# Four graph layers on one core: the last layer in groups of four blocks, shorter ends of the gathering passes, and the last product in rows

## What is computed

```
h = relu(layernorm(x)); x = x + layer0(h)  # sum of neighbours, product 256->512, batch norm, relu, product ->256, batch norm, relu
h = relu(layernorm(x)); x = x + layer1(h)  # two weighted sums over edges (in and out), gates
h = relu(layernorm(x)); x = x + layer2(h)  # sum of neighbours, products 256->256->256 with batch norms
h = relu(layernorm(x)); x = x + layer3(h)

# layer3, for each edge (src, tgt):
feat = concat(x[tgt], x[src] - x[tgt])
hid  = relu(feat @ W1 + b1)                # 512 wide
msg  = hid @ W2 + b2                       # 256 wide
out  = segment_sum(msg, tgt) / (deg + 1e-8)
```

## Time and profile before

| | us |
|---|---|
| median of three runs | 3542.32 |
| the profiled execution | 3547.39 |
| its span | 3545.6 |
| TensorE matmul busy | 2770.3 (78%) |
| GpSimd busy | 2368.3 (67%) |
| VectorE busy | 2055.5 (58%) |
| ScalarE busy | 1146.7 (32%) |

### The profile page before, as it was taken

How to read it: one execution, slowest core, us unless ns; L and a number is a source line. 1 busy time by engine, 2 the same in 40 slices (tenths; PEclk the granted TensorE clock), 3 DMA queues, 4 the chain that set the end, 5 groups by cost and what they waited for, 6 DMA issues and landing times.

```text
span 3545.6 us, 57073 instructions
## 1 busy us (share of the span) xinstructions
PE 2770.3 (78%) x12116; PEld 1910.4 (54%) x12117; DVE 2055.5 (58%) x6142; ACT 1146.7 (32%) x3033; POOL 2368.3 (67%) x2444
## 2 busy tenths in 40 slices
PE   4999866666875766667999676666668889999999
PEld 2444444444434444445777444444444469999996
DVE  7999833443455544445444546444444488888883
ACT  1999700000142010000000014000003457777772
POOL 5777777777777777777777733777771046666661
PEclk6999977777886777877999887777778899999999
DMA  4000033333214333333333313333331157777774
GB/s 146 2 2 2 3 105 104 104 104 104 59 41 153 97 105 104 104 106 105 104 104 102 104 51 95 105 104 104 105 104 30 66 172 214 214 210 216 213 215 127
DMA packets 168186, 381.37 MB, mean 108 GB/s; under 512 B 53443, under 2 KB 78094, under 8 KB 168131
## 3 DMA queue, kind: packets, MB, share of 16 engines
q0 software_dynamic: 123264, 321.84, 31.6%
q1 hardware_dynamic: 44867, 58.89, 5.0%
HBM read 352.65 MB, written 27.84 MB: 107 GB/s over the span
## 4 chain that ended last, share of the span: by engine, by line
PE 44%; issue 22%; POOL 16%; DMA 11%; DVE 4%; DVEq 1%; ACT 1%; POOLq 0%; ACTq 0%; SPq 0%
PE psum L1926 17%; PE psum L2189 11%; POOL acc L771 9%; POOL recs L747 7%; DMA acc<-table,stg_idx 6%; PE psum L2177 6%; PE psum L2101 4%; DMA recs<-acc,sst_idx 3%; PE psum L1947 2%; DVE acc L1336 1%; DVEq L528 1%; PE psum L2146 1%; DMA recs<-acc 1%; DVE oh L1325 1%; PE psum L2128 1%
## 5 line engine op out<-in xcount | busy, mean ns | idle before, releaser
L771 POOL DMA_INDIRECT acc<-table,stg_idx x1568 | 1501.3, 957 | 492.9 <-issue 437.7
L1926 PE MATMUL psum<-acc,oh 128*128 x3520 | 1228.5, 501 | 595.6 <-SPq L611 266.3
L1926 PEld LDWEIGHTS psum<-acc,oh 128*128 128x128 f32 x3520 | 817.2, 248 | 987.1 <-issue 857.4
L1336 DVE TENSOR_TENSOR acc<-acc,psum 128x257 f32 (+1 forms) x880 | 371.3, 422 | 889.5 <-PE psum L1926 881.5
L921 ACT CAST stg_idx<-rec 128x2 int32 (+1 forms) x784 | 149.3, 193 | 1790.2 <-PE psum L1926 1766.3
L841 POOL DMA_INDIRECT TT<-qtable,stg_row x440 | 419.8, 954 | 188.8 <-issue 166.2
L1327 DVE TENSOR_SCALAR oh<-iota,stg_lw 128x128 f32<-128x128 f32 x1320 | 404.3, 363 | 133.1 <-issue 133.0
L2189 PEld LDWEIGHTS psum<-oh,TT 128*128 128x128 f32 x3520 | 427.9, 192 | 19.4
L2189 PE MATMUL psum<-oh,TT 128*128 128x128 f32 x3520 | 429.0, 275 | 0.0
L747 POOL DMA_INDIRECT recs<-acc,sst_idx x290 | 305.4, 1053 | 120.1 <-issue 86.0
L1996 PE MATMUL psum<-H 125*128 125x440 bf16 x1600 | 314.0, 350 | 14.5 <-ACT H L874 13.2
(11 more groups left out here) (256 smaller groups left out, 2571.4 us busy)
## 6 DMA issues: line engine op xcount, KB each, us to landing
acc<-table,stg_idx POOLq DMA_INDIRECT x1568
table<-H SPq DMA_DIRECT2D x12, 640.0 KB
TT<-loc_dram SPq DMA_DIRECT2D x22, 320.0 KB, 5.1
TT<-qtable,stg_row POOLq DMA_INDIRECT x440
Wm<-loc_dram SPq DMA_DIRECT2D x22, 320.0 KB, 4.9
qtable<-H SPq DMA_DIRECT2D x24, 256.0 KB, 2.0
recs<-acc,sst_idx POOLq DMA_INDIRECT x290, 2.1
recs<-rec SPq DMA_DIRECT2D x5, 880.0 KB, 5.7
```

Source lines behind the costliest of these rows:

```text
L771: pool.indirect_dma_start(out=dst[:, c, 0:D], out_offset=None, in_=src, in_offset=bass.IndirectOffsetOnAxis(ap=stg_idx[:, c:c + 1], axis=0 ...
L1336: V.tensor_tensor(at, at, sum_bank(j)[:, 0:w], ALU.add).then_inc(added, 1)
L1926: last = mm(sum_bank(j)[:, 0:w], oh[:, 2 * j + k, :], rows_flat[:, ds(start[j] + k * S, w)], start=(k == 0), stop=(k == 1))
```

## The change

Three parts. (1) The last turn of each narrow pass is written out; its last pair of gathers is one gather of END_ROWS = 80 rows, and `relay` and its counts follow. (2) The norm of layer 3, its transposes, the q products and the addition of the bias go in groups of four blocks, interleaved in the programs of TensorE, VectorE and ScalarE; all 25 q blocks come before the p blocks; back2 has banks 3, 4 and 5; the second memset of H is cut into three, of which two (5376 columns) run once q is stored and one (1024 columns) after the last p block. (3) "down3" and "back3" give way to "out3": H is the stationary operand and W2 the moving one, so that a result is a block in rows, 25 x 4 matmuls of 256 columns; ScalarE's copies go.

```
 def relay(n):
-    with sp.Fori(n * GITS, (n + 1) * GITS) as i:
+    short = [0] * (RING_G - 1) + [16]
+    with sp.Fori(n * GITS, (n + 1) * GITS - 1) as i:
         for j in range(RING_G):
-            sp.wait_ge(landed[j], i * 32 + 32)
+            sp.wait_ge(landed[j], i * 32 + (32 - n * short[j]))
             sp.sem_inc(arrived, 1)
+    for j in range(RING_G):
+        sp.wait_ge(landed[j], (n + 1) * GITS * 32 - (n + 1) * short[j])
+        sp.sem_inc(arrived, 1)
 # GpSimd, gathers(n, src, dst)
-    with pool.Fori(n * GITS, (n + 1) * GITS) as i:
+    with pool.Fori(n * GITS, (n + 1) * GITS - 1) as i:
         for j in range(RING_G):
             gather_pair(i, j, src, dst)
+    for j in range(RING_G - 1):
+        gather_pair((n + 1) * GITS - 1, j, src, dst)
+    pool.wait_ge(staged, (n + 1) * GITS * RING_G)
+    pool.sem_inc(stages_begun, 1)
+    c = 2 * RING_G - 2
+    pool.indirect_dma_start(out=dst[0:END_ROWS, c, 0:D], out_offset=None, in_=src,
+        in_offset=bass.IndirectOffsetOnAxis(ap=stg_idx[0:END_ROWS, c:c + 1], axis=0)
+    ).then_inc(landed[RING_G - 1], 16)
 # GpSimd, clearing H
-    all_filled("p3")
-    nc.gpsimd.memset(Hm[:, NB * D:4 * NP], 0.0).then_inc(sums_clear, 1)
+    all_filled("q3")
     for q in range(QS):
         pool.wait_ge(q_stored[q], 16 * (NB // QS))
+    p_half = w0 + 2 * HID
+    nc.gpsimd.memset(Hm[:, NB * D:w0], 0.0).then_inc(sums_clear, 1)
+    nc.gpsimd.memset(Hm[:, p_half:4 * NP], 0.0).then_inc(sums_clear, 1)
+    all_filled("p3")
+    nc.gpsimd.memset(Hm[:, w0:p_half], 0.0).then_inc(sums_clear, 1)
 # ScalarE
+    for g in range(len(TG) + 3):
+        n = 2 * (NB // GROUP) + g + 2
+        if g < len(TG): deviations(n, 4 * g, len(blocks_of(g)))
+        if 1 <= g <= len(TG): norm_blocks(n - 1, 4 * (g - 1), len(blocks_of(g - 1)))
+        if 2 <= g <= len(TG) + 1: take_transpose(3, g - 2)
+        if g >= 3:
+            for t in blocks_of(g - 3): take_q(t)
 # VectorE
+    for g in range(len(TG) + 2):
+        n = 2 * (NB // GROUP) + g + 2
+        if g < len(TG): ln_rows(blocks_of(g), "back2").then_inc(ln_var, 1)
+        if 1 <= g <= len(TG):
+            done = blocks_of(g - 1)
+            ln_scale(n - 1, slice(done.start, done.stop))
+        if g >= 2:
+            take_transpose(3, g - 2)
+            full_rows(blocks_of(g - 2))
 # TensorE
+    back_rows(0)
+    back_rows(1)
     for g in range(len(TG) + 1):
+        if g + 2 < len(TG): back_rows(g + 2)
         if g < len(TG): transpose_group(3, g)
         if g >= 1:
             for k in (0, 1): wait_emptied(pe, "T3", 2 * (g - 1) + k)
-        for t in blocks_of(g - 1):
-            if t < Q_FIRST: rows_product("q3", t, 2)
+            for t in blocks_of(g - 1): rows_product("q3", t, 2)
     pe.wait_ge(wdiff, 1)
     for t in range(NB):
         rows_product("p3", t, 0)
-        if Q_FIRST + t < NB: rows_product("q3", Q_FIRST + t, 2)
...
-    for n in range(NT):
-        products("down3", n, 2, [(W2e[:, k, :], H_at(k, n)) for k in range(4)], n * 2)
-        back("back3", u_ready, lambda n: NT + 2 * (n + 1), ended_by(n - 1))
-    back("back3", u_ready, lambda n: NT + 2 * (n + 1), ended_by(NT - 1))
+    for t in range(NB):
+        r = rows(t)
+        dst = take_bank("out3", t)
+        for k in range(4):
+            last = mm(dst[0:r, 0:D], H[:, k, t * P:t * P + r], W2e[:, k, :], start=(k == 0), stop=(k == 3))
+        done(last, "out3", t)
```

More of the change, by code:

```diff
@@ L35 @@
 HB = 2
+END_ROWS = E - (GROUPS - 1) * EDGES
+assert 0 < END_ROWS <= P and END_ROWS % 16 == 0
 assert EP * EC == E and CHUNKS % (2 * CH_IT) == 0 and CHUNKS % 4 == 0 and CH_IT % HB == 0
@@ L62 @@
 MID = N // 2
-Q_FIRST = 16
 PFS = 3
@@ L502, in gnn_kernel @@
         plan("down2", 2 * NT)
-        plan("back2", NB)
+        plan("back2", NB, (3, 4, 5))
         plan("T3", 2 * len(TG), (6, 7))
@@ L506, in gnn_kernel @@
         plan("p3", NB, (3, 4, 5))
-        plan("down3", 2 * NT, range(4))
-        plan("back3", NB, range(4, 8))
+        plan("out3", NB)
         def blocks_of(g):
@@ L1057, in take_q @@
                 nc.scalar.copy(qst[0:rows(t), t % QS, :], src[0:rows(t), :]).then_inc(emptied[bank("q3", t)], 1)
-            for g in range(len(TG) + 1):
+            for g in range(len(TG) + 3):
+                n = 2 * (NB // GROUP) + g + 2
                 if g < len(TG):
-                    take_transpose(3, g)
-                for t in blocks_of(g - 1):
-                    if t < Q_FIRST:
+                    deviations(n, 4 * g, len(blocks_of(g)))
+                if 1 <= g <= len(TG):
+                    norm_blocks(n - 1, 4 * (g - 1), len(blocks_of(g - 1)))
+                if 2 <= g <= len(TG) + 1:
+                    take_transpose(3, g - 2)
+                if g >= 3:
+                    for t in blocks_of(g - 3):
                         take_q(t)
@@ L1256, in ln_stats, with ln_rows @@
             def ln_stats(g, back=None):
+                return ln_rows(range(g * GROUP, (g + 1) * GROUP), back)
+            def ln_rows(blocks, back):
                 stats = []
-                for t in range(g * GROUP, (g + 1) * GROUP + 2):
-                    if back is not None and t < (g + 1) * GROUP:
+                for t in range(blocks.start, blocks.stop + 2):
+                    if back is not None and t < blocks.stop:
                         add_back(back, t)
-                    if g * GROUP <= t - 1 < (g + 1) * GROUP:
+                    if t - 1 in blocks:
                         r = rows(t - 1)
@@ L1268, in ln_stats @@
                         stats.append(nstep[0])
-                    if g * GROUP <= t - 2:
+                    if t - 2 in blocks:
                         r = rows(t - 2)
-                        dve.wait_ge(vstep, stats[t - 2 - g * GROUP])
+                        dve.wait_ge(vstep, stats[t - 2 - blocks.start])
                         last = V.bn_aggr(lnmv[0:r, t - 2, :], lnst[0:r, (t - 2) % (2 * GROUP), :])
@@ L1301, in add_back, with take_transpose @@
                     emptied[bank(st, t)], 1)
+            def take_transpose(layer, g):
+                st = f"T{layer}"
+                src = wait_filled(dve, st, 2 * g + 1)
+                n = min(512, N - 512 * g)
+                V.tensor_copy(TT[:, 1, 512 * g:512 * g + n], src[:, 0:n]).then_inc(emptied[bank(st, 2 * g + 1)], 1)
             def take_transposes(layer):
@@ L1684, in _, with full_rows @@
             bn_scale(5, 2, "L2_gnn_g2", "L2_gnn_be2")
[L1685 to L1695, removed]
+            def full_rows(blocks):
+                dve.wait_ge(b1_loaded, 32)
+                dve.wait_ge(rdeg_ready, 1)
+                dve.wait_ge(normed, 3 * NB + blocks.stop)
+                for t in blocks:
+                    r = rows(t)
+                    V.scalar_tensor_tensor(xt[0:r, t, :], b2bc[0:r, :], full_col[0:r, t:t + 1], xt[0:r, t, :], ALU.mult,
+                                           ALU.add).then_inc(x_full, 1)
+            for g in range(len(TG) + 2):
+                n = 2 * (NB // GROUP) + g + 2
+                if g < len(TG):
+                    ln_rows(blocks_of(g), "back2").then_inc(ln_var, 1)
+                if 1 <= g <= len(TG):
+                    done = blocks_of(g - 1)
+                    ln_scale(n - 1, slice(done.start, done.stop))
+                if g >= 2:
+                    take_transpose(3, g - 2)
+                    full_rows(blocks_of(g - 2))
+            wait_emptied(dve, "T3", 2 * len(TG) - 2)
+            wait_emptied(dve, "T3", 2 * len(TG) - 1)
             dve.wait_ge(merged, SPLIT - 1)
@@ L2139, in _, with back_rows @@
             down("down2", W2c, 2, 8 * NT)
-            back("back2", act_ready, lambda n: 10 * NT + 2 * (n + 1))
+            def back_rows(g):
+                back("back2", act_ready, lambda n: 10 * NT + 2 * (n + 1), blocks_of(g))
+            back_rows(0)
+            back_rows(1)
             def rows_product(st, t, w):
@@ L2158, in _ @@
                         wait_emptied(pe, "T3", 2 * (g - 1) + k)
-                for t in blocks_of(g - 1):
-                    if t < Q_FIRST:
+                    for t in blocks_of(g - 1):
                         rows_product("q3", t, 2)
```

25 lines of the change are left out of this document (11 added, 14 removed).

## The result

The kernel after takes 3515.39 us (median of four runs, 3512.74 to 3516.25), the kernel before, on the same chip, 3542.43 (four runs, 3540.14 to 3544.27). The ratio is 0.9923, with a 95% interval of 0.9906 to 0.994. The gain is 27.0 us; forecast were 24.3 and a time of 3518.

What follows compares the result with a forecast made beforehand. No engine bounds the whole (TensorE 44% of the chain). Gains of 5.8 (passes), 12.7 (groups and what follows the products) and 5.8 (last product) sum to 24.3: 3547.4 - 24.3 = 3523.1, less 5.07: 3518 us; range 3510 to 3530.

Steps and rivals of the forecast that it cites:

- Pass ends: End of the four aggregation passes: removed gathers save 5.0 us, fewer rows 0.8; gain 5.8, from 0.3 to 7.9.
- Rival E: At the pass ends, written-out tails cost what the gathers saved; with groups also chaining, gain 10 in all, 3532 us; 4%.
- Groups, to the first product: Last layer, first back transpose to first q product: 10.5 us less, the product starting at 2762.0 instead of 2772.5.
- The wait: Group 3's fourth back block waits for VectorE's add until about 2759.8; group 1's transposes and the first product queue behind.
- rival B: After the p products: gather's start decides, VectorE blocked less, clock at 2.4 GHz from back transposes; total gain 30.2, 3512; 15%.
- Hand-over: Last p product to first spread: 9.5 us becomes 8.9 (9.5 - 3.9 + 0.5 + 2.8), 0.6 less.
- VectorE's lag: At the p blocks, early memsets block VectorE; it begins 1.9 to 2.8 us late and stays so.
- TensorE is not stopped: Among the p products TensorE, three banks ahead, has slack of 2.74 us, so VectorE's lateness does not stop it.
- The wait and the warm work: Hidden loop's start: TensorE's 0.9 us wait for the first join goes, cold work turns warm (at most 1.7); 1.5 forecast.
- Last product: Kernel's end, product in rows: 200 instructions at 0.218 us make 43.6; 49.5 - 43.7 gives gain 5.8, from 1.4 to 6.5.
- Rival C: In the last product each weight load stands alone: 7.5 us lost against the 5.8; total gain 16.8, 3525.5 us; 5%.
- Rival D: Last layer's row products stay at 1.2 GHz, 1.717 us more per block; with all 25 q blocks 18.6 slower, 3561; 4%.

Runs made afterwards that it cites:

- e_pass: The kernel before with only the pass ends changed (one gather of 80 rows for the last two, last turn written out); 3533.85 us, ratio 0.9977.
- e_bias: The kernel after with VectorE adding the last layer's bias rows four groups later; 4327.59 us, on a chip where the kernel before takes 4367.
- e_whole: The kernel after with columns 6400 on of the hidden sums cleared by one memset after the last p product, as before; 3515.83 us, ratio 0.9924.

## Why the prediction was right, and where a term was off

- **Pass ends** (5.8). The stages give 7.0, and e_pass alone 6.9. The removed issue is exact (1.26 a pass, with 391 gathers for 392), the 48 rows are 0.25 for 0.2, and the written-out turn costs nothing. The remaining 1.0 is within the scatter of passes 1 and 2 and has no cause that a run shows. Rival E is out.
- **Groups, to the first product** (10.5). It gave 10.5 where the clock was still low at the second group's transposes, 11.6 where it was at 2.4 GHz by then. The wait is where it was put: the fourth block was forecast for 2759.8, that is 2750.2 once the 9.6 us are taken off by which the back transposes start earlier, and came at 2749.87; e_bias shows its cause. What the forecast left out is that the clock may have risen again before the first product: it was low at the first group's transposes, but in four of the nine traces with this order it was high at the second group's (1.04 us for eight, not 1.91). That is a part of rival B.
- **Hand-over** (0.6 forecast, 1.75 measured). The mis-sized term of the sum. The prediction took VectorE's lag at its upper end, 2.8, and added 0.5 for the short memset. The lag at VectorE's last p block was 2.1, by e_whole against after, and the short memset held nothing. With these, 9.5 - 3.9 + 2.1 = 7.7, as measured. The mechanism was right: doubled, it stops TensorE; removed, it gives 2.1. Only "TensorE is not stopped" was not quite so: it lost 0.46 us among the p products.

  The Trainium skill, "SBUF — State Buffer", section SBUF: two separate sides, says that GpSimd and VectorE share a pair of ports as an exclusive lock, held for the whole instruction by whichever comes first, and that VectorE needs the pair in its two-port modes, or with two SBUF inputs only against a GpSimd operation that reads SBUF. The traces agree: a memset, which reads nothing, held a one-source instruction for up to 4.34 us and left two-source ones at 0.69. That the held instruction runs in such a two-port mode is taken from its behaviour; no row names the mode.
- **What decides the start of the loop.** The prediction said the spread, B the gather. The join waits for the spread (2.27 us, for TensorE). With gather and spread later by 4.7 and 1.8 us only 1.5 arrive, so it isn't the gather's start that decides. The wait and the warm work, for which 1.5 were forecast, gave 0.4. That this forecast was 1.1 too high and that of the hand-over 1.15 too low is luck: the two errors cancel in the sum.
- **Last product** (5.8). 43.57 us for 200 instructions, 5.9 gained to the last finish. Rival C is out: no weight load stands alone.
- **Rival D** didn't occur: every group of products after the first ran at full clock.

By the stages the forecast's 5.8 + 12.7 + 5.8 read 7.0 + 12.7 to 14.4 + 5.8, and the untouched stage adds 0.6 by chance.

## What to carry to other kernels

Price a change by stages, and take each stage's scatter from several traces: here a pass pair scatters by 5 us, as much as one part is worth. Before moving a piece of work behind another, name what stands behind it on each engine: one block moved back, to save 0.4 us in each group, cost 4.2. When GpSimd clears memory, choose a time when VectorE runs no instruction like L1749 here, or let an idle ScalarE do it.

## What the runs showed of the hardware

- On one chip the kernel before took 23% longer (4367 us for 3541). In four traces from there single instructions are, at the same clock, as long as elsewhere (a gather 958 to 961 ns on average for 957); the waits between them are longer, in the loops and in the written-out stage behind pass 0 (189 to 249 us for 144), while the norm and the products of the last layer, also written out, took the same time to 0.2 us. The cause was not looked for.
- An indirect gather of 80 rows takes 0.907 us to issue, one of 128 rows 0.957: the rows hardly count.
- A stop of 4.05 us of TensorE in a dense stage lengthened it by 6.1: the granted clock was 0.88 and 0.84 in two windows of 6 us in a row, the first of which begins within the stop, and 1.00 behind them.
